# Vision tower with a mixture of experts: the low part of each weighted unit on GpSimd in place of VectorE

## What is computed

```python
logits = xf @ Wr.T + br                      # 2080 tokens, 8 experts
probs = softmax(logits); top2_prob, top2_idx = top_k(probs, 2)
comb = zeros((n, 8)).at[arange(n)[:, None], top2_idx].add(top2_prob)
h = gelu(einsum('nd,edh->enh', xf, W1) + b1[:, None, :])      # 128 -> 256
o = einsum('enh,ehd->end', h, W2) + b2[:, None, :]            # 256 -> 128
y = einsum('ne,end->nd', comb, o)                             # weighted sum over experts
```

## Time and profile before

| | before |
|---|---|
| median of 3 runs | 251.25 us (250.98 to 252.55) |
| span of the profiled execution, first to last instruction | 249.9 us |
| what the median has beside that span | 1.35 us |
| TensorE matmul / weight load busy | 230.9 / 194.7 us |
| VectorE busy | 191.3 us |
| ScalarE busy | 164.2 us |
| GpSimd busy | 62.8 us, none after 144 us |

### The profile page before, as it was taken

One profiled execution on the slowest core, in us unless ns is written; L12 is line 12 of the kernel. 1 busy time (PEld: TensorE's weight loads), 2 busy tenths in 40 slices (PEclk: granted clock), 3 DMA queues, 4 the chain that ended last, 5 costly groups with the idle time before them and its releaser, 6 DMA issues.

```text
span 249.9 us, 6298 instructions
## 1 busy us (share of the span) xinstructions
PE 230.9 (92%) x2316; PEld 194.7 (78%) x2316; DVE 191.3 (77%) x481; ACT 164.2 (66%) x509; POOL 62.8 (25%) x94
## 2 busy tenths in 40 slices
PE   1999999999998889989989999999899999999993
PEld 1945665899776766658778899889799999999972
DVE  1576789865668899998186738678999989989991
ACT  2461469752199899993026987422799888898870
POOL 8814132096005465469112400000000000000000
PEclk9999999999999999999999999999999999999999
DMA  6980000000003326064000000069888510001011
GB/s 147 335 217 3 1 0 1 3 3 0 3 0 81 91 65 108 4 212 129 3 7 3 0 3 0 8 103 131 151 211 260 173 37 10 22 4 32 0 42 34
DMA packets 15625, 16.46 MB, mean 66 GB/s; under 512 B 1747, under 2 KB 14367, under 8 KB 15468
## 3 DMA queue, kind: packets, MB, share of 16 engines
q1 hardware_dynamic: 14424, 15.59, 26.0%
q0 software_dynamic: 544, 0.35, 0.6%
q10 hardware_dynamic: 628, 0.14, 0.3%
HBM read 13.91 MB, written 2.16 MB: 64 GB/s over the span
## 4 chain that ended last, share of the span: by engine, by line
PE 54%; DVE 13%; issue 11%; POOL 11%; DMA 4%; ACT 3%; SPq 2%; DVEq 0%; POOLq 0%
PE banks L1328 49%; POOL region_e L471 5%; DMA region_d<-in_L_tok_W_sw 4%; DVE KT L1286 2%; POOL w_lo L526 2%; DVE top L1028 1%; DVE stb L992 1%; POOL region_d L478 1%; PE banks L1531 1%; POOL rstd L413 1%; PE banks L1672 1%; DVE stb L911 1%; ACT region_d L701 1%; DVE y_lo L1269 1%; DVE stats L890 1%
## 5 line engine op out<-in xcount | busy, mean ns | idle before, releaser
L760 ACT ACTIVATE w_sb<-banks,vecs 128x416 f32<-128x416 f32 x60 | 36.4, 608 | 11.2 <-PE banks L1328 8.9
L677 ACT ACTIVATE region_e<-banks,ntop 128x64 f32<-128x64 f32 x128 | 38.3, 346 | 5.0 <-DVE ntop L1035 4.8
L768 ACT ACTIVATE y_hi<-w_sb 128x416 fp32r<-128x416 f32 x60 | 32.7, 548 | 8.1 <-DVE w_sb L1260 8.1
L1269 DVE TENSOR_TENSOR y_lo<-w_sb,y_hi 128x416 fp32r<-128x416 f32 x60 | 34.9, 585 | 1.0 <-ACT y_hi L768 1.0
L677 ACT ACTIVATION_READ_ACCUMULATOR region_e<-banks,ntop 128x1 f32 x128 | 29.8, 238 | 0.0
L1328 PE MATMUL banks<-x_hi,w_hi 128*128 128x416 f32 x80 | 29.3, 366 | 0.0
L1328 PE MATMUL banks<-x_lo,w_hi 128*128 128x416 f32 x80 | 28.1, 352 | 0.0
L1328 PE MATMUL banks<-x_hi,w_lo 128*128 128x416 f32 x80 | 28.0, 350 | 0.0
L1260 DVE TENSOR_TENSOR w_sb<-w_sb,region_c 128x416 f32<-128x416 f32 x40 | 23.4, 586 | 2.5 <-ACT w_sb L760 1.0
L1328 PE MATMUL banks<-y_hi,w_hi 128*128 128x416 f32 x60 | 22.3, 371 | 1.5 <-DVE KT L1286 1.0
L1328 PE MATMUL banks<-y_hi,w_lo 128*128 128x416 f32 x60 | 21.1, 351 | 0.0
(11 more groups left out here) (238 smaller groups left out, 502.1 us busy)
## 6 DMA issues: line engine op xcount, KB each, us to landing
region_c<-out SPq DMA_DIRECT2D x4, 832.0 KB, 14.3
xnT<-out SPq DMA_DIRECT2D x5, 208.0 KB, 13.7
QT<-out SPq DMA_DIRECT2D x5, 208.0 KB, 14.1
region_a<-in_x SPq DMA_DIRECT2D x2, 512.0 KB, 5.3
region_a<-in_x SPq DMA_DIRECT2D x1, 1024.0 KB, 9.5
out<-h SPq DMA_DIRECT2D x2, 512.0 KB, 5.8
h<-out SPq DMA_DIRECT2D x4, 256.0 KB, 5.0
w_sb<-in_L_ffn_W SPq DMA_DIRECT2D x1, 1024.0 KB, 5.6
```

The lines of the kernel that those rows point to most:

```text
L677: last = a.activation(dst[:, h // 2, h % 2], src[:, h // 2, h % 2], ACT.Exp, scale=SCALE, bias=ntop[:, o + h:o + h + 1], accum_out=esum[:, ...
L760: a.activation(lifted(u), bank[h_bank(i)][:, 0:FB], ACT.Gelu, bias=vecs[:, b:b + 1])\
L768: a.activation(h_hi(u), lifted(u), ACT.Copy).then_inc(S["hi_ok"], 1)
L1269: v.tensor_tensor(h_lo(u), lifted(u), h_hi(u).bitcast(F32), ALU.subtract).then_inc(S["lo_ok"], 1)
```

## The change

`rest(u)` for all 60 units moves from VectorE's program to the end of GpSimd's, with the same three waits and the same signal. VectorE keeps `weigh`, in the same order, and `joined`. Nothing else is edited.

```diff
         @block.gpsimd
             deviation2(3)
             deviation2(4)
 
+            def rest(u):
+
+                pool.wait_ge(S["hi_ok"], u + 1)
+                pool.wait_ge(S["hs_ok"], u + 1)
+                if u >= H_RING:
+                    pool.wait_ge(S["y3_ps"], (u - H_RING) // 2 + 1)
+                g.tensor_tensor(h_lo(u), lifted(u), h_hi(u).bitcast(F32), ALU.subtract).then_inc(S["lo_ok"], 1)
+
+            for u in range(LATER):
+                rest(u)
+
...
-            def rest(u):
-
-                dve.wait_ge(S["hi_ok"], u + 1)
-                dve.wait_ge(S["hs_ok"], u + 1)
-                if u >= H_RING:
-                    dve.wait_ge(S["y3_ps"], (u - H_RING) // 2 + 1)
-                v.tensor_tensor(h_lo(u), lifted(u), h_hi(u).bitcast(F32), ALU.subtract).then_inc(S["lo_ok"], 1)
-
...
                     if (e, g) == (1, 3):
                         weigh(2)
-                        rest(0)
...
             for u in range(3, LATER):
-                if u > 3:
-                    rest(u - 3)
                 weigh(u)
                 if u >= 20 and u % 12 == 8:
                     joined((u - 20) // 12)
-            for u in range(LATER - G_RING + 1, LATER):
-                rest(u)
             joined(4)
```

## The result

The changed kernel takes 264.25 us (263.48 to 265.01, four runs) against 251.12 us for the kernel before on the same chip: 1.052 times, 95% interval 1.048 to 1.056. It is slower by 13 us; forecast were 10.5 us more and 261.7 us, with a range of 255 to 269. Some executions of any of these kernels run a per cent or more longer with nothing changed; the ratios and the ranges of the kernel before leave these out.

What follows compares the result with a forecast made beforehand. TensorE, at 1.13 us a unit, was taken as the bound before; 56 alternating units at 1.365 us (76.4 us) and three subtractions alone (3.2 us) put 10.5 us on the span, giving 261.7 us, range 255 to 269.

Steps and rivals of the forecast that it cites:

- the collision: In the stage, VectorE's weighting and GpSimd's subtraction exclude each other and alternate, near 1.365 us a unit; chance 0.80.
- four meetings: Places in the earlier trace where operations of GpSimd and VectorE overlap and wait, counted as four of four against no collision.
- Its price: Cost of one alternating unit: 0.455 us for VectorE's weighting plus 0.91 us for GpSimd's subtraction, 1.365 us.
- the interpolation: Estimate of one 416-column subtraction alone on GpSimd from lines 526 and 431: 1.08 us, where 1.06 was taken.
- What is hidden: Start of the waiting operation that overlaps the other engine's: 0.13 us on VectorE, 0.15 us on GpSimd.
- The Trainium skill's handover: Blocked GpSimd going on 115 ns after VectorE's end: 1.63 us a unit and 276.5 us; the prediction judged the rows against it.
- The sum: First subtraction ends about 175.0 us, 56 alternating units take 76.4, three alone 3.2; the last ends at 254.6 us.
- The five additions: Line 1307 on VectorE, reading one SBUF tile beside GpSimd: costed at nothing, 2.8 us at most.
- No collision: Rival: GpSimd's 1.06 us and the two-unit loop of 2.22 us fit under TensorE's pace, 250.5 to 252 us; chance 0.08.
- Faster: Rival: VectorE's relief ends TensorE's 2.9 us of load waits for the low part, 248.4 us; chance 0.04.
- Dearer: Rival: nothing of GpSimd's start hidden, 1.515 us a unit, 270 us; nothing hidden at all, 277; chance 0.08.
- The clock's rival: A waiting TensorE might be granted 1.2 in place of 2.4 GHz; chance 2 in 100, within the dearer case.

Runs made afterwards that it cites:

- experiment 3: The changed kernel with a fill with zeros on GpSimd in place of the subtraction: 249.98 us, one run, where the kernel before ran at 251.7 to 255.3.
- experiment 10: The kernel before with Gelu written back to PSUM and weighted there, low parts of even units on GpSimd, odd ones on VectorE: 0.992 of the kernel before.
- experiment 1: The changed kernel with the weighting, from unit 3 on, multiplying by a PSUM bank's contents, turned sums using one bank less: 1.006 of the kernel before.
- experiment 2: The changed kernel with six lifted tiles in place of four: 1.048 of the kernel before.
- experiment 5: The changed kernel, whole layer, with the lift writing its Gelu back to the PSUM bank and the weighting reading it there: 1.012 of the kernel before.
- experiment 7: The changed kernel with the weighting as a product with a constant: 255.51 us, one run, where the kernel before ran at 250.5 to 252.6.

## Why the prediction was right, point by point

*The bound before and the cover.* TensorE at 1.13 us a unit was the bound, with the two others just below. Where the collision is gone and GpSimd's load small (experiments 3 and 10), the time comes back to that of before or just under it.

*The collision.* The meetings in the trace of before were enough to name it, and experiments 1, 2 and 5 show it against its rivals: taking away the second SBUF input cures it, more tiles don't. The prediction counts four meetings and tells three. A fourth is there, line 1004 on VectorE, 0.38 us beside a copy where its median is 0.169; but another one, of line 1168 with a power on GpSimd, hardly shows (usual are 0.69 and 1.01 us), so "four of four" said too much (each time GpSimd, then VectorE, in the kernel before):

```profile
79.68 0.40 POOL L478 COPY region_d<-rel_rows 128x256 f32<-128x256 f32 x1
...
142.29 1.04 POOL L532 TENSOR_TENSOR rstd<-ve,mhalf 32x1 f32<-32x1 f32 x1
```

```profile
79.73 0.38 DVE L1004 TENSOR_TENSOR esum<-esum,spc 128x16 f32<-128x16 f32 x1
...
142.23 0.69 DVE L1168 TENSOR_TENSOR x_lo<-QT,x_hi 128x512 fp32r<-128x512 f32 x1
```

Of the operations that the prediction calls untouched "with one SBUF input", the copies of line 1049 have none (they read a PSUM bank), and experiment 7 shows one with a single SBUF input that is touched.

*Its price.* Forecast was 0.455 + 0.91 = 1.365 us a unit; measured are 0.45 and 0.94 to 0.95, 1.39. The term that was mis-sized is the subtraction alone: 1.06 us were taken where the interpolation itself gave 1.08, and it is 1.08 to 1.09. What is hidden, 0.13 and 0.15 us, held: 0.585 - 0.45 and 1.09 - 0.94. The Trainium skill's handover ("SBUF — State Buffer", section "A bandwidth-pool intuition that's wrong (but worth ruling out)"), 115 ns after VectorE's end, was measured there on a DMA whose descriptors GpSimd writes. Taken for these operations, by the prediction's estimate, it would have made the unit 1.63 us; the trace does not agree, at 1.39.

*The sum.* The last subtraction ended at 255.24 + 1.08 = 256.3 us, forecast 254.6: 56 x 0.028 = 1.6 us more by the unit's price; 0.7 us more because only the last subtraction ran free and not the last three (the two ahead of it took 2.80 us together from 252.48 us on, VectorE's last weighting between them); 0.5 us less because the first began earlier. The five additions, costed at nothing, cost nothing that shows. Once a block, four times, GpSimd waits 0.24 us for a rounding, but from one such wait to the next twelve units take 16.71 us, 1.39 each as elsewhere (timeline of GpSimd):

```profile
192.88 16.47 POOL L550 TENSOR_TENSOR y_lo<-w_sb,y_hi 128x416 fp32r<-128x416 f32 x12 [0.24 <-ACT y_hi L779]
209.59 16.47 POOL L550 TENSOR_TENSOR y_lo<-w_sb,y_hi 128x416 fp32r<-128x416 f32 x12 [0.23 <-ACT y_hi L779]
```

The end after TensorE took some 0.3 us more than before, with a lower granted clock (last section). The profiled execution lasted 264.28 us beside a span of 262.4, 1.9 us more, where 1.35 was taken from the median before. The later last subtraction (1.7 us), the longer end (0.3) and this distance (0.5) make the 2.5 us between 261.7 and 264.25.

*The rivals.* "No collision" asked for 250.5 to 252 us; without the collision experiments 1 and 5 took 1.006 and 1.012, or 252.6 to 254.1 us by the 251.12 of before. It forgot the drain: three subtractions after the last weighting at 1.07 us (six in 6.45 in experiment 5) in place of 0.50, 1.7 us. "Faster" came in experiment 10, by 0.8% or 2.1 us, of the 2.9 that were counted for VectorE's relief. That the relief is what gives them is not shown: in the one profile of it, of a run of 253.31 us, the weight loads still wait 2.8 us for the low part.

```profile
PEld banks L1338 <- DVE y_lo L1280: 1.5, 2, 1.1
...
PEld banks L1338 <- POOL y_lo L550: 1.3, 2, 0.9
```

"Dearer" did not come. The clock's rival was told for the stage, where it stayed 1.00.

## What to carry to other kernels

Before moving an operation from VectorE to GpSimd, add up, operation by operation, the time for which each will keep the other waiting (here an operation of GpSimd that reads SBUF and one of VectorE with two SBUF inputs, or a product with a constant from SBUF to SBUF), and set that sum against the stage's pace, not GpSimd's duration alone: here 1.08 us fitted under 1.13, and 1.39 did not. Put an operand of VectorE's operation in PSUM to take it out of that sum, leave VectorE a part of the work, and let the quicker engine do the last units of a drain. To find such a collision in a trace, lay the two engines' timelines side by side and look for durations above those of the same form elsewhere.

## What was not expected of the hardware

That VectorE's product with a constant waits behind GpSimd (0.362 to 1.26 us, experiment 7) was not read from the kernel before, whose trace has a hint of it: line 413, a power of 128x4 on GpSimd, took 1.20 and 1.17 us beside products of this form (line 919, 128x512), 1.01 and 1.03 us the other two times.

And the granted clock fell at the end of the changed kernel (the last two stretches):

```profile
250.00:255.00 5.00, 3.45 (x14) 2.04 (x13) 4.34 (x5) 3.04 (x6) 5.00 (x4) 1.00 0.23 54
255.00:262.40 7.40, 2.58 (x10) 1.49 (x10) 0.74 (x2) 0.52 (x1) 1.32 (x2) 0.70 0.11 29
```

A mean of 0.70 is part of the stretch at 2.4 and the rest at 1.2 GHz. Ahead of it TensorE had been busy 3.45 of 5 us; before, a stretch with 3.97 of 5 busy kept 1.00. The kernel before kept 1.00 to its end, though TensorE was busy only 0.61 us of its last 4.9. What the lower clock costs is seen in the chain on the three transposes behind the stage, 0.65 us where they took 0.34 before:

```profile
258.10 0.65 PE banks L1834 x3
```

```profile
245.89 0.34 PE banks L1836 x3
```

The spans of the four runs went with the clock, 261.6 us at a mean of 1.000 and 263.2 at 0.985, but on another chip the kernel before had spans from 249.8 to 253.4 us all at 1.000, so these 1.6 us are not shown to come from it.
